# Low half of the shared down weights on GpSimd, a later slot norm, rank products in fp32r

## The reference, cut

```python
x = L0_attn_x                                            # (16, 256, 256)
x = _layernorm(x + attn(x))        # q, k, v, g; decay-masked q k^T v; a norm per head; silu(g) * . @ w_o
# ffn:
logits = x @ router_w.T                                  # the largest one picks the token's expert
xr = x[None] * sigmoid(score)                            # zero for the experts not taken
gate, up = jnp.split(jnp.einsum('eth,ehf->etf', xr, gate_up_proj), 2, axis=-1)
routed = jnp.einsum('etf,efh->eth', up * jax.nn.silu(gate), down_proj)
shared = jax.nn.silu(x @ shared_gate_w) * (x @ shared_up_w) @ shared_down_w
x = _layernorm(x + shared + routed.sum(axis=0))
```

## Time and profile before

| | before |
|---|---|
| median of 3 executions | 569.64 us (569.25 to 569.81) |
| profiled execution, its own time | 572.99 us |
| its span | 570.9 us |
| PE busy | 548.1 us, 96% of the span |
| DVE, POOL, ACT busy | 419.4, 321.5, 232.8 us |
| share of PE in the chain that ended last | 77% |

### The profile page before, as it was taken

The page is one execution under the profiler, slowest core; times in us unless marked ns, Lnnn a source line. Parts: engine busy times, 40 slices in busy tenths (PEclk is TensorE's granted clock), DMA queues, the critical chain, the costliest instruction groups (busy, mean ns, idle before and its releaser), DMA issues.

```text
span 570.9 us, 11864 instructions
## 1 busy us (share of the span) xinstructions
PE 548.1 (96%) x3888; PEld 458.5 (80%) x3888; DVE 419.4 (73%) x865; ACT 232.8 (41%) x411; POOL 321.5 (56%) x319
## 2 busy tenths in 40 slices
PE   7998989999999999999999899999999999999994
PEld 5776769779779779779778587888888888888883
DVE  5888986978977977977966687757855666666664
ACT  3434433364363363364353765133333233333331
POOL 0544493295296296297294283726666656566644
PEclk9999998999999999999999999999999999999998
DMA  7902205703707607706374623765676666665651
GB/s 256 306 9 75 75 0 42 220 0 43 218 1 151 218 3 150 218 4 157 126 273 172 221 91 111 241 206 173 195 169 163 211 190 195 189 197 182 193 176 37
DMA packets 46506, 83.55 MB, mean 146 GB/s; under 512 B 11585, under 2 KB 30529, under 8 KB 46433
## 3 DMA queue, kind: packets, MB, share of 16 engines
q1 hardware_dynamic: 38736, 64.27, 39.1%
q0 software_dynamic: 6048, 15.39, 8.9%
q10 hardware_dynamic: 1664, 3.15, 1.5%
HBM read 60.85 MB, written 22.34 MB: 146 GB/s over the span
## 4 chain that ended last, share of the span: by engine, by line
PE 77%; DVE 7%; issue 4%; POOL 4%; DMA 4%; ACT 1%; POOLq 0%; DVEq 0%; ACTq 0%
PE duo L1588 44%; PE duo L1965 8%; PE duo L1810 6%; PE duo L1644 5%; DMA out_rows<-of,seat 4%; PE duo L1666 4%; PE duo L1975 2%; PE duo L1854 1%; PE duo L1814 1%; PE duo L1748 1%; PE duo L1800 1%; POOL turned L901 1%; POOL rstd L918 1%; PE duo L1790 1%; PE duo L1706 1%
## 5 line engine op out<-in xcount | busy, mean ns | idle before, releaser
L1588 PE MATMUL duo<-w_gu_hi,xsT 128*128 x312 | 107.4, 405 | 0.0
L1588 PE MATMUL duo<-x1T,wsgu 128*128 128x512 f32 x384 | 93.2, 395 | 0.0
L1588 PEld LDWEIGHTS duo<-x1T,wsgu 128*128 128x128 f32 x384 | 71.0, 188 | 15.3
L901 POOL TENSOR_TENSOR turned<-turned,swapped 128x1024 f32<-128x1024 f32 x16 | 38.4, 2423 | 67.5 <-DVE swapped L1094 67.5
L1032 POOL DMA_INDIRECT out_rows<-of,seat x39 | 39.6, 1016 | 59.7 <-DMA out_rows<-of,seat 42.4
L1588 PEld LDWEIGHTS duo<-w_gu_hi,xsT 128*128 128x128 f32 x312 | 58.7, 188 | 11.5
L1527 DVE SCALAR_TENSOR_TENSOR eh<-duo,seat,e_act 128x512 f32<-128x512 f32 x39 | 29.3, 751 | 45.5 <-PE duo L1588 45.5
L1588 PE MATMUL duo<-w_gu,xsT 128*128 x156 | 60.8, 390 | 0.0
L1103 DVE TENSOR_TENSOR sims<-duo,causal 128x512 f32<-128x512 f32 x64 | 41.2, 686 | 15.9 <-ACT sims L662 15.8
L1965 PE MATMUL duo<-w_dn,ehT 128*128 x156 | 47.2, 303 | 3.5 <-DVE ehT_lo L1535 3.5
L1023 POOL DMA_INDIRECT xz<-xz_d,seat x39 | 45.2, 1159 | 9.2 <-issue 8.3
(11 more groups left out here) (178 smaller groups left out, 1280.9 us busy)
## 6 DMA issues: line engine op xcount, KB each, us to landing
dn_rest<-dn_lo_d SPq DMA_DIRECT2D x39, 512.0 KB, 4.4
w_gu<-L_ffn_gate_up_proj SPq DMA_DIRECT2D x8, 1024.0 KB, 8.2
x_in<-x_t SPq DMA_DIRECT2D x8, 512.0 KB, 8.3
x_res<-L_attn_x SPq DMA_DIRECT2D x8, 512.0 KB, 4.3
dn_raw<-L_ffn_down_proj SPq DMA_DIRECT2D x8, 512.0 KB, 7.5
xz_d<-zs SPq DMA_DIRECT2D x8, 512.0 KB
dn_hi_d<-dn_top SPq DMA_DIRECT2D x8, 512.0 KB, 6.4
dn_lo_d<-dn_low SPq DMA_DIRECT2D x8, 512.0 KB, 6.4
```

Of the source, the lines that this page charges most:

```text
L901: nc.gpsimd.tensor_tensor(turned[:, g, :, :], turned[:, g, :, :], swapped[:, g, :, :], ALU.add)\
L1588: last = mm(out_, left(a, k), right(b, k), start=start and k == 0 and n == 0, stop=stop and k == kt - 1 and n == len(PASSES) - 1)
```

## The change

1. The low half of `wsd_s` moves from DVE (L1449 drops out of turn 2) to POOL, ahead of `turn(2, 0)`.
2. In turn 2 POOL does `group_rstd(1)` between `turn(2, 0)` and `turn(2, 1)`, no longer behind both.
3. `PARTED` no longer has turn 2: expert 0's down weights are split in turn 3 together with expert 1's, as turns 4 to 6 do for theirs.
4. In the slot loop of DVE, `slot_norm(s-2)` goes behind `slot_sum(s-1)` and `hidden_lo(s)`.
5. `before`, `ones` and `hot` become fp32r, so the two rank products do. The tables land in a corner of `x1` and ACT copies them in turn 1 (two more ACTIVATE of 128x128). A new semaphore `counts_ok` holds ACT's first write of `x1` and PE's first `rank` until then.

```diff
-PARTED = {2: (0,), 3: (1,), 4: (2, 3), 5: (4, 5), 6: (6, 7)}
+PARTED = {3: (0, 1), 4: (2, 3), 5: (4, 5), 6: (6, 7)}
...
-        before = sb("before", [P, P])
-        ones = sb("ones", [P, P])
+        before = sb("before", [P, P], F32R)
+        ones = sb("ones", [P, P], F32R)
...
-        hot = sb("hot", [P, TILES, EXPERTS])
+        hot = sb("hot", [P, TILES, EXPERTS], F32R)
...
             def first_norm(f):
 
                 act.wait_ge(sig.nmr_ok, f + 1)
+                if f == 0:
+                    act.wait_ge(sig.counts_ok, 2)
...
                         act.wait_ge(sig.r_in, 16 * N_IN)
+                        for n, exact in enumerate((before, ones)):
+                            nc.scalar.activation(exact[:, :], x1[:, 0, n * P:(n + 1) * P], ACT.Copy).then_inc(sig.counts_ok, 1)
                         act.wait_ge(sig.w_lo, 4)
...
+            def shared_down_rest():
+                pool.wait_ge(sig.wsd_hi, 1)
+                nc.gpsimd.tensor_tensor(wsd_s[:, 1, :, :], wsd[:, :, :], f32(wsd_s[:, 0, :, :]), ALU.subtract)\
+                    .then_inc(sig.wsd_lo, 1)
...
                 if has(f) and t <= PAIRS:
                     norm_scales(f)
+                if t == 2:
+                    shared_down_rest()
                 if has(t):
                     turn(t, 0)
...
+                    if t == 2:
+                        group_rstd(a)
                     turn(t, 1)
                 if has(a):
-                    group_rstd(a)
+                    if t != 2:
+                        group_rstd(a)
                     residual(a)
...
-                if t == 2:
-                    dve.wait_ge(sig.wsd_hi, 1)
-                    nc.vector.tensor_tensor(wsd_s[:, 1, :, :], wsd[:, :, :], f32(wsd_s[:, 0, :, :]), ALU.subtract)\
-                        .then_inc(sig.wsd_lo, 1)
                 if has(t + 1):
                     x_lo(t + 1)
...
                 rows_lo(s + 1)
-                if is_slot(s - 2):
-                    slot_norm(s - 2)
                 if is_slot(s - 1):
                     slot_sum(s - 1)
                 if is_slot(s):
                     hidden_lo(s)
+                if is_slot(s - 2):
+                    slot_norm(s - 2)
...
             def rank(f):
 
                 pe.wait_ge(sig.hot_ok, f + 1)
+                if f == 0:
+                    pe.wait_ge(sig.counts_ok, 2)
```

More of the change, by code:

```diff
@@ L355, in build @@
             route = new("route")
+            counts_ok = new("counts_ok")
             hot_ok = new("hot_ok")
@@ L486, in _ @@
             sp.dma_start(wsd[:, :, :], sh_down.rearrange("(k p) n -> p k n", p=P)).then_inc(sig.r_in, 16)
-            sp.dma_start(before[:, :], squares[:, 2 * P:3 * P]).then_inc(sig.r_in, 16)
-            sp.dma_start(ones[:, :], squares[:, 3 * P:4 * P]).then_inc(sig.r_in, 16)
+            sp.dma_start(x1[:, 0, 0:P], squares[:, 2 * P:3 * P]).then_inc(sig.r_in, 16)
+            sp.dma_start(x1[:, 0, P:2 * P], squares[:, 3 * P:4 * P]).then_inc(sig.r_in, 16)
             sp.dma_start(priority[:, :], squares[:, 4 * P:4 * P + EXPERTS]).then_inc(sig.r_in, 16)
@@ L1332, in choose @@
                 dve.wait_ge(sig.route, at(ROUTE * p + 3))
-                nc.vector.tensor_tensor(ranked[:, :, :], hot[:, :, :], over(priority[:, :], TILES), ALU.mult)\
+                nc.vector.tensor_tensor(ranked[:, :, :], f32(hot[:, :, :]), over(priority[:, :], TILES), ALU.mult)\
                     .then_inc(sig.route, 1)
@@ L1358, in find_seats @@
                 dve.wait_ge(sig.hot_ok, at(p + 1))
-                nc.vector.tensor_tensor(spot[:, :, :], spot[:, :, :], hot[:, :, :], ALU.mult).then_inc(sig.route, 1)
+                nc.vector.tensor_tensor(spot[:, :, :], spot[:, :, :], f32(hot[:, :, :]), ALU.mult).then_inc(sig.route, 1)
                 dve.wait_ge(sig.route, at(ROUTE * p + 12))
```

## The result

| | before | changed |
|---|---|---|
| median | 570.19 us (569.13 to 571.68, 20 executions) | 567.35 us (566.74 to 570.96, 20) |
| ratio | | 0.995, 95% interval 0.994 to 0.996 |
| profiled execution, its own time | 572.99 us | 567.32 us |
| its span | 570.9 us | 565.4 us |
| PE, DVE, POOL busy | 548.1, 419.4, 321.5 us | 545.1, 415.3, 322.6 us |

The change gains 2.84 us (2.3 to 3.4 by the interval), where 4.8 had been forecast. The median of 564.8 us that was forecast started from 569.64 us, the median of three executions. Twenty have 570.19, so 0.55 of the 2.6 us by which it was off lie in where it started. Compare also the last times with the medians. The profiled execution of the changed kernel took 567.32 us, its median to 0.03 us. That of before took 572.99, nearly 3 us over its median of 570.19. So the two profiles differ by 5.7 us, and the kernels by 2.84.

A forecast was written before the change was run, and what follows sets the result against it. PE was taken to bound the kernel, busy 96% of the span. Stall -1.6, clock -1.7, rank -1.5, slots -2.1 and tail +2.1 sum to -4.8 us: 569.64 to 564.8 us, range 562.3 to 567.9.

The forecast's parts named there:

- 567.8: Rival, turn 2: the second rotation takes the stall's place, stall shrinks by 0.3 us, clock falls as before; chance 0.16.
- 566.9: Rival, slots: they keep their stall, since landings move with the later issue and POOL is late by as much; chance 0.10.
- the last subtraction: Sum: profiled execution from 572.99 to 568.2 us; median, taken as 3.35 lower, from 569.64 to 564.8 us.
- Stall in turn 2: PE's wait at `shared_down(0)`: start at 83.8 in place of 85.45, 1.6 us gained; bounds 0 and 2.6.
- Clock: Behind turn 2's stall: the granted clock no longer falls, `shared_down` 5.75 instead of 7.47 us, 1.7 gained; bounds 0 and 1.7.
- Expert 0's split in turn 3: Turns 2 and 3: moving the split costs PE's chain nothing; bounds 0 and +0.5 us.
- Rank products: PE's `rank` in the turns: fp32r saves 0.22 us each, seven count, 1.5 us gained; bounds 0 and 1.6.
- The fourth rival: Rank products: fp32r is not cheaper at 32 columns, 566.3 us; chance 0.10.
- Slots: Slot loop: the later norm removes PE's stalls after late scatter landings, 2.1 us gained; bounds 0 and 2.7.
- Tail: Last slots: the later norm delays the last scatter from 567.45 to 569.5, 2.1 us lost; bounds 1.3 and 3.0.
- Rival 5: From 443 us on the scatter chain becomes the period of 26 slots; 572.9 us at spacing 5.3; chance 0.06.

The follow-up runs named there:

- slot_only: The kernel before with only `slot_norm` moved behind `hidden_lo` in the slot loop; 572.83 us, ratio 1.0041.
- tail_only: The kernel before with `slot_norm` moved behind `hidden_lo` in the last three steps of the slot loop alone; 572.48 us, ratio 1.0032.
- spread_seats_c: The kernel before with the last pair's seat scatters in steps 7, 9, 11 and 13, late seats loaded two steps later; 570.81 us, ratio 0.9994.
- wsd_parted: The kernel before with the low half of `wsd_s` on POOL and expert 0's split in turn 3, scales behind both rotations; 568.58 us, ratio 0.9969.
- rstd_only_c: The kernel before with only turn 2's scales moved between the two rotations; 571.83 us, ratio 1.0027.
- turn2_only: The kernel before with `wsd_s` low half on POOL, scales between the rotations and expert 0's split in turn 3; 566.76 us, ratio 0.9939.
- rank_only: The kernel before with only the rank products made fp32r; 569.19 us, ratio 0.9985.
- tail_fixed: The changed kernel with `slot_norm` back in its old place in the last three steps of the slot loop; 564.56 us, ratio 0.9899.
- no_slot: The changed kernel with the slot loop of before, `slot_norm` ahead of `slot_sum` and `hidden_lo`; 566.18 us, ratio 0.9914.

## Why the prediction was right, and why it was 2.6 us off

It said 564.8 us, 562.3 to 567.9, and faster with 0.88. The direction was right, and 567.35 lies in the range, near its upper end. Two rivals named times nearby, 567.8 and 566.9, but neither happened: PE no longer stands at `shared_down(0)`, and the slots lost their stalls in the profile.

**The step that failed is the last subtraction.** The sum was made against the profiled execution, 572.99, and its distance of 3.35 us from the median was carried over as a constant. For the profiled execution the forecast was 568.2, and 567.32 was measured. But the distance was no constant. The second profile of before, with 569.59, shows that the first one had 1.5 us of fallen clock and 1.8 us of slot stalls more. These are parts of the very terms that I then took off the median. Of the 3.4 us between the two profiled executions the median of 20 (570.19) holds 0.6, and the medians beside the experiments (570.59 to 571.02) 1.0 to 1.4. An edit can take off the median only what the middle execution has.

**Stall in turn 2: predicted 1.6, measured 2.5.** The four profiles with edits 1 to 3 start `shared_down(0)` at 82.76 to 83.23, 83.04 in the mean; the five with the old turn 2 whole (before twice, `slot_only`, `tail_only`, `spread_seats_c`) at 85.33 to 85.65, 85.51 in the mean. The chain went as written: the subtraction at 62.13, the scales done at 76.77 (forecast 77.0), the norms 77.18 to 78.46, the rotation until 79.15, `x_res` behind it. Of the 0.6 us between 83.8, the forecast, and 83.18 in the changed kernel's profile, about half is that `h_low(1)` ended at 79.70, not 80.05. The rest is the 0.35 us added for a longer hold of the product in `find_seats`, which didn't come: from `h_low(1)` to PE's start it is 3.48 us, with `spot` at 0.81, and 3.4 before. There is nothing left to gain, as PE comes free at 83.12.

The three parts don't add. Edits 1 and 3 gain 1.0 us of the start (`wsd_parted`), edit 2 alone loses 0.5 (`rstd_only_c`), and all together gain 2.5. What edit 2 is worth depends on what POOL has behind the scales.

Each hold in these rows ends with a POOL instruction on two arrays in SBUF. The scales do not hold: DVE's `hT_lo` at 75.17 took its usual 0.69 us in the middle of POOL's 5.80 us of `rstd`. The Trainium skill (SBUF — State Buffer, "SBUF: two separate sides") lets a GpSimd operation keep the shared port pair for its whole length against a VectorE operation with two SBUF inputs. For `x_res` and the rotations the traces agree: 2.27 us behind `x_res`, 1.32 and 2.26 behind a rotation, for a product of 0.69. For `dn_low` they agree too, with 0.76 us in the kernel before for the product on `spot`, which takes 0.19 in `wsd_parted`. For `rstd` they don't, and the measurement decides.

**Clock: predicted 1.7, measured 1.5 where it happens and nothing where it doesn't.** Seven profiles have a stall of 2.3 us or more. In four the clock fell and `shared_down` took 7.47 or 7.48 us, behind stalls of 2.3 to 2.9 us. In three it took 5.98 or 5.99 and the windows show 1.00, behind 2.4 to 2.6 us. The size is 7.47 - 5.98 = 1.49, not 7.47 - 5.75: I had compared with turn 3, but in turn 2 the products take 0.23 us more than there at the full clock too. At four in seven the term is worth 0.85 us in the mean. None of the five profiles with a stall under 1.2 us shows the fall, which is the part of the step that held.

Each timed execution has its mean granted clock on record too. Of the 63 of the kernel before beside the experiments, 21 have 0.998 or 0.999 and a median of 569.59 us, 29 have 0.995 or less and a median of 571.37, and 13 lie between. That mean counts the whole span, so it points to the fall in turn 2 and does not prove it. If it is the fall, about half of the executions or more have it, and the median of a group can lie among them. Then it holds the whole 1.5 us, as the 3.8 us of `turn2_only` suggest.

**Expert 0's split in turn 3: predicted nothing, nothing in turn 3.** From `shared_down(0)` to (1) the kernels with and without it take 43.20 (changed) and 43.19 us (`rank_only`). The gain in turn 2 was missed, as said.

**Rank products: predicted 1.5, by the rows 1.3.** A turn is 0.18 us shorter, not 0.22. The fourth rival is out. The ratio alone (0.9 us, and up to 0.2 the other way) would not have shown it.

**Slots: predicted 2.1, 1.2 in the mean of the profiles.** In the profile pair it is 2.7 us, as the bound said. But the nine profiles with the old order through the middle lose 2.7, 0.9, 3.0, 0.9, 1.9, 0.8, 0, 0.5 and 0.4 us to steps over the usual (in the order of the table), 1.2 in the mean, and the three with the late norm nothing. I took the size of one execution for that of the kernel. By times the late norm alone, without its tail, is worth 1.6 us by the medians and 0.9 by the ratios (`tail_fixed` against `no_slot`); between `slot_only` and `tail_only`, which ran in different groups, nothing shows. In the first pair five of the six times of `tail_fixed` lie under all six of `no_slot`, but the two intervals overlap, and the second pair shows no sign. So I leave the size at 0 to 1.6.

**Tail: predicted 2.1 lost, measured 2.41.** The mechanism was right in each part: norm(36) behind `hidden_lo(38)`, scatters 3.3 us apart from there on, and slot 38's scale behind scatter(37). Scatter(36) starts 2.56 us behind the transpose of slot 38's `eh` instead of 0.15, which is 2.41, and 2.44 was the forecast. The size was lost at the last gap, for which I took 2.9 us and which is 3.30 like the others. `tail_only` has the same 9.16 us. In the kernels with the old order at the end four of nine tails are longer than 6.7 us, by 0.5 to 1.5, so against their mean of 7.1 the loss is 2.1.

**Together:** -2.5 for the stall, -0.85 clock, -1.3 rank, -1.2 slots, +2.4 tail, a sum of -3.5 us, against -2.84 (2.3 to 3.4). The three parts by their own times, -3.8, -1.4 and +2.2, give -3.0. The 0.6 us that are left no run here assigns, and with the whole 1.5 us for the clock they would be 1.3. The clock and the slots are the terms with room. Between the two profiled executions without a fall in turn 2 (before again, 569.59, and changed, 567.32) it is 2.27 us.

That the forecast came as near as it did has some luck in it. The stall was taken 0.9 us too small, and that covered part of what the clock (0.85), the slots (0.9), `rank` (0.2) and the tail (0.3) had too favourably.

**Rival 5** did not happen: the scatter chain never became the period. The slots took 184.2 us, within 0.1 of the least of all, with 1.14 us of DVE idle left in the step shown.

**Open.** What makes POOL stand 2.5 to 5.4 us for the landing of a scatter in some executions and steps, and what decides whether the clock falls behind the same stall. Two profiles of one kernel differ in both, so both would take many profiles.

## What to carry to other kernels

Compare the profiled execution's own time with the median before subtracting anything from the median: where it is dearer, some of its stalls are that execution's own, and a second profile of the unchanged kernel shows which. It also takes more than three executions to say what the median is when they fall into groups. A step that is moved behind another in a loop is free in the middle and dear in the last rounds, where a chain of landings hangs on it; give the last rounds their old order. When two engines hold each other, price what stands back to back after the move, not each instruction alone.

## What the runs showed of the hardware

- The granted clock fell behind a PE stall of 2.3 to 2.9 us in four profiles and stayed at 1.00 behind 2.4 to 2.6 us in three, with nearly the same instructions around it. Here are the unfallen and a fallen case, `before` again and `slot_only`, both with a stall of 2.4 us (columns as above):

```profile
85.00:90.00 5.00, 4.52 (x38) 4.55 (x39) 4.27 (x8) 3.23 (x5) 3.59 (x5) 1.00 0.02 5
```

```profile
85.00:90.00 5.00, 4.67 (x26) 4.70 (x27) 4.17 (x7) 3.23 (x5) 3.60 (x5) 0.66 0.03 5
```

  In the same 5 us PE got through 38 matmul instructions in the one and 26 in the other.
- A DVE cast of 128x4 with one input was held for 1.85 us (2.02 instead of 0.17) until POOL's subtraction of 128x1024 had ended, while DVE's product of 128x512 ran at full pace (0.69 us) beside POOL's `rstd`. The other way round, POOL's `var_e` of 128x32 took 1.21 us instead of 0.30 beside DVE's subtraction of 128x1024.
- Dependent scatters of 128 rows never started closer than 3.27 us in the twelve profiles. At a slot step of 4.85 us they keep up on the whole.
- The second product of `rank`, an fp32r matmul with 32 columns, adds 0.11 us to PE's chain, half of the plain fp32 one (0.22 for two instructions). Both products together add 0.13 instead of 0.36, and a turn is 0.18 us shorter.
